# The second mixture's last 32 rows of each expert's output on four column tiles, then one summing product

## The reference

```python
gates = softmax(xf @ Wg.T);  topw, topi = top_k(gates, 2)
C = int(round(K * T * CAP_RATIO / E))          # 2 * 2048 * 1.05 / 8 = 538
...                                            # the first C tokens that chose an expert go to its buffer
h = gelu(einsum('ecd,edh->ech', buf, W1) + b1[:, None, :], approximate=False)
y = einsum('ech,ehd->ecd', h, W2) + b2[:, None, :]
...                                            # each token sums its two results, weighted by topw
```

## Time and profile before

| | us |
|---|---|
| Median of 3 runs | 2809.65 |
| Lowest and highest | 2803.67, 2810.41 |
| The profiled execution | 2807.44 |
| Its span, first to last instruction | 2806.2 |
| TensorE matmul busy in it | 2396.2 |
| VectorE, ScalarE, GpSimd busy | 1209.0, 882.0, 555.6 |

### The profile page before, as it was taken

One profiled execution on the slowest core, in us unless ns is written; L12 is line 12 of the kernel. 1 busy time (PEld: TensorE's weight loads), 2 busy tenths in 40 slices (PEclk: granted clock), 3 DMA queues, 4 the chain that ended last, 5 costly groups with the idle time before them and its releaser, 6 DMA issues.

```text
span 2806.2 us, 33074 instructions
## 1 busy us (share of the span) xinstructions
PE 2396.2 (85%) x13070; PEld 1626.3 (58%) x13070; DVE 1209.0 (43%) x2227; ACT 882.0 (31%) x2384; POOL 555.6 (20%) x553
## 2 busy tenths in 40 slices
PE   5786999938995879787999999599957899768999
PEld 5674777726773655223566657477743588623555
DVE  5753222175887563565333311300025466655220
ACT  1211222233671441553222221122214355213220
POOL 1621222234001011111344410222221100022100
PEclk9977999969997989998999999699977899979999
DMA  4006888530001000200000000322226433100000
GB/s 157 0 31 243 304 302 307 219 111 1 2 2 50 1 1 30 95 1 30 0 1 0 0 1 5 125 87 90 84 87 267 194 135 133 61 4 1 8 8 15
DMA packets 75376, 224.12 MB, mean 80 GB/s; under 512 B 9359, under 2 KB 52757, under 8 KB 65238
## 3 DMA queue, kind: packets, MB, share of 16 engines
q1 hardware_dynamic: 67894, 204.76, 20.1%
q0 software_dynamic: 7328, 17.26, 1.8%
HBM read 178.61 MB, written 45.17 MB: 80 GB/s over the span
## 4 chain that ended last, share of the span: by engine, by line
PE 48%; DVE 7%; DMA 2%; ACT 1%; POOL 1%; issue 1%; SPq 0%; POOLq 0%; DVEq 0%; ACTq 0%
PE psum L221 27%; PE psum L3246 6%; PE psum L2289 2%; PE psum L3255 2%; PE psum L2276 2%; PE psum L1786 2%; PE psum L1791 2%; DMA positions<-arena 2%; PE psum L1802 1%; DVE stats L253 1%; PE psum L1817 1%; DVE arena L2336 1%; PE psum L2506 1%; POOL small L2704 1%; PE psum L404 1%
## 5 line engine op out<-in xcount | busy, mean ns | idle before, releaser
L221 PE MATMUL psum<-arena 128*128 128x256 f32 (+6 forms) x4100 | 1046.6, 413 | 26.3 <-DVE arena L3342 13.1
L221 PEld LDWEIGHTS psum<-arena 128*128 128x128 f32 (+2 forms) x4100 | 723.8, 184 | 305.4 <-issue 136.5
L263 POOL TENSOR_SCALAR x_moments<-x_moments 128x4 f32<-128x4 f32 x48 | 12.0, 250 | 919.6 <-DVE x_moments L256 919.1
L1876 DVE TENSOR_REDUCE small<-psum 128x4 f32<-128x1024 f32 (+1 forms) x112 | 137.0, 1223 | 112.9 <-PE psum L1791 65.3
L3246 PE MATMUL psum<-arena 128*128 128x512 bf16 x768 | 166.4, 379 | 0.0
L1224 POOL DMA_INDIRECT l_out<-arena,slot_tables x79 | 78.7, 996 | 441.4 <-ACT arena L1397 233.6
L1851 ACT ACTIVATE arena<-psum,small 128x128 f32<-128x128 f32 (+1 forms) x384 | 148.9, 417 | 49.2 <-DVE small L1876 49.0
L1416 DVE TENSOR_TENSOR arena<-arena,psum 128x352 f32<-128x352 f32 x78 | 40.7, 521 | 253.3 <-ACT arena L1375 253.3
L1887 DVE COPY arena<-psum 128x512 f32<-128x512 f32 x224 | 143.6, 681 | 1.8 <-PE psum L1802 1.5
L404 PE MATMUL psum<-ident,z 128*128 128x128 f32 x256 | 48.1, 349 | 107.2 <-DVE z L274 76.7
L1786 PE MATMUL psum<-arena 32*128 32x128 f32 (+1 forms) x1280 | 133.4, 339 | 0.0
(11 more groups left out here) (334 smaller groups left out, 3389.2 us busy)
## 6 DMA issues: line engine op xcount, KB each, us to landing
arena<-L_ffn_w_in SPq DMA_DIRECT2D x39, 2176.0 KB, 8.8
arena<-L_ffn_W_in SPq DMA_DIRECT2D x16, 1024.0 KB
positions<-arena SPq DMA_DIRECT2D x16, 1024.0 KB, 6.0
arena<-positions SPq DMA_DIRECT2D x16, 1024.0 KB, 8.2
arena<-l_out SPq DMA_DIRECT2D x16, 512.0 KB, 7.3
positions<-arena SPq DMA_DIRECT2D x16, 512.0 KB, 6.5
arena<-positions SPq DMA_DIRECT2D x16, 512.0 KB, 9.0
arena<-ctx_in SPq DMA_DIRECT2D x2, 2048.0 KB, 10.1
```

Source lines behind the costliest of these rows:

```text
L221: last = nc.tensor.matmul(out, lhsT, rhs, start=(n == 0), stop=(n == len(pairs) - 1))
L1876: nc.vector.reduce_max(self.minus_top(h), use.bank(u).rearrange("p (h l) -> p h l", l=L), AX_X, negate=True).then_inc(self.topped.up(), 1)
```

## The change

The last output group of 26 rows is no longer computed as 8 products one on top of the other. In its place there are, for each expert:

- **`pe_strips(e)`**, ahead of the four full groups: 8 products for the rows 506 to 537 (32 rows, so six of the fourth group's rows are computed here too and not used). Column tile s takes the hidden tiles 2s and 2s + 1, a quarter of the features, and writes partitions 32s to 32s + 31 of one bank. The tile index is innermost.
- **A copy by ScalarE** of that bank (128 x 256) to `strips`, in two buffers by turns.
- **One summing product** behind the fourth full group: the stationary operand is `same_row`, four 32 x 32 identities on top of each other, from which the last 26 columns are taken; the moving operand is `strips`. It adds the four quarters for each of the 26 rows. VectorE adds the bias to its result as before.

`same_row` is built once, by three small additions on GpSimd at the start of the stage. Each expert now books 26 uses of PSUM instead of 25.

```diff
+        tail = k.arena[:, 4 * SLAB + 2 * 4352 + E * D:4 * SLAB + 2 * 4352 + E * D + 2 * D + 32]
+        self.strips, self.same_row = [tail[:, D * n:D * n + D] for n in (0, 1)], tail[:, 2 * D:]
+        self.folded = k.counter("same_row_made", "pool").reserve(1)
...
                 self.turn_use.append([u.add("dve", 2), u.add("act", 2)])
+            self.strip_use.append(u.add("act"))
             self.y_use.append([u.add("dve") for _ in range(RT)])
...
             pe.wait_ge(*use.emptied(self.h_use[e][1][-1]))
-            for a, u in enumerate(self.y_use[e]):
-                n = self.count(a)
-                products(nc, use.take(u)[0:n, 0:D], [(self.hid[e % 2][:, m, P * a:P * a + n], w2[:, m, :])
-                                                     for m in range(MT)]).then_inc(use.fills(u), 1)
+            self.pe_strips(e)
+            for a, u in enumerate(self.y_use[e][:-1]):
+                products(nc, use.take(u)[:, 0:D], [(self.hid[e % 2][:, m, P * a:P * a + P], w2[:, m, :])
+                                                   for m in range(MT)]).then_inc(use.fills(u), 1)
+            u, n = self.y_use[e][-1], self.count(self.RT - 1)
+            pe.wait_ge(self.folded)
+            pe.wait_ge(*use.emptied(self.strip_use[e]))
+            nc.tensor.matmul(use.take(u)[0:n, 0:D], self.same_row[:, 32 - n:32], self.strips[e % 2],
+                             start=True, stop=True).then_inc(use.fills(u), 1)
...
+    def pe_strips(self, e):
+        nc, use, u, per = self.k.nc, self.uses, self.strip_use[e], self.MT // 4
+        bank = use.take(u)
+        for j in range(per):
+            for s in range(4):
+                mm = nc.tensor.matmul(bank[32 * s:32 * s + 32, 0:D], self.hid[e % 2][:, per * s + j, CAPACITY - 32:CAPACITY],
+                                      self.w2[e % 2][:, per * s + j, :], start=(j == 0), stop=(j == per - 1))
+        mm.then_inc(use.fills(u), 1)
...
             self.empty_turn(e + 1, "act")
+            u = self.strip_use[e]
+            act.wait_ge(*use.filled(u))
+            if e >= 2:
+                act.wait_ge(*use.filled(self.y_use[e - 2][-1]))
+            copied(k, "act", self.strips[e % 2], use.bank(u)[:, 0:D]).then_inc(use.empties(u), 1)
...
     def pool(self):
+        rows = [k.ident[:, 32 * s:32 * s + 32] for s in range(4)]
+        pool.step(k.nc.gpsimd.tensor_tensor(self.same_row, rows[0], rows[1], ALU.add))
+        pool.step(k.nc.gpsimd.tensor_tensor(self.same_row, self.same_row, rows[2], ALU.add))
+        k.nc.gpsimd.tensor_tensor(self.same_row, self.same_row, rows[3], ALU.add).then_inc(self.folded.up(), 1)
         self.load_rows(0)
         self.load_rows(1)
```

More of the change, by code:

```diff
@@ L2763, in __init__ @@
         self.router = Router(k, u, self.norm, self.fetch.loaded, E * RT, CAPACITY, False)
-        self.turn_use, self.h_use, self.y_use = [[u.add("dve", 2), u.add("act", 2)]], [], []
+        tail = k.arena[:, 4 * SLAB + 2 * 4352 + E * D:4 * SLAB + 2 * 4352 + E * D + 2 * D + 32]
+        self.strips, self.same_row = [tail[:, D * n:D * n + D] for n in (0, 1)], tail[:, 2 * D:]
+        self.folded = k.counter("same_row_made", "pool").reserve(1)
+        self.turn_use, self.h_use, self.y_use, self.strip_use = [[u.add("dve", 2), u.add("act", 2)]], [], [], []
         for e in range(E):
@@ L2866, in pool @@
     def pool(self):
-        pool = self.k.pool
+        k, pool = self.k, self.k.pool
+        rows = [k.ident[:, 32 * s:32 * s + 32] for s in range(4)]
+        pool.step(k.nc.gpsimd.tensor_tensor(self.same_row, rows[0], rows[1], ALU.add))
+        pool.step(k.nc.gpsimd.tensor_tensor(self.same_row, self.same_row, rows[2], ALU.add))
+        k.nc.gpsimd.tensor_tensor(self.same_row, self.same_row, rows[3], ALU.add).then_inc(self.folded.up(), 1)
         self.load_rows(0)
         self.load_rows(1)
-        pool.wait_ge(self.k.zeroed)
+        pool.wait_ge(k.zeroed)
         for e in range(E):
```

## The result

| | before | changed |
|---|---|---|
| Median, us | 2808.30 | 2789.02 |
| Lowest and highest, us | 2803.67, 2810.41 | 2784.72, 2791.30 |
| The profiled execution's span, us | 2806.2 | 2788.3 |

The ratio is 0.9932, 95% interval 0.9914 to 0.9950, or 19.3 us by the medians. 2793 with a range of 2786 to 2801 was forecast. Both intervals hold the 16.1 us of the sum; the first, 14.0 to 24.2 us, cannot tell 16.1 from 19.3.

What follows compares the result with a forecast made beforehand. TensorE was taken to bound the kernel; 1.01 + 0.43 - 3.45 = -2.01 us an expert, -16.1 us over eight, gave 2791.4 us from the profile and 2793.6 from the median, stated as 2793, range 2786 to 2801.

Steps and rivals of the forecast that it cites:

- the sum: Per expert in the second mixture, 1.01 + 0.43 - 3.45 = -2.01 us; over eight experts -16.1 us.
- Steps 1 to 3: Per expert on TensorE: strips add 1.01 us, the summing product adds 0.43, the removed narrow group takes away 3.45.
- The signs: Marks expected in the profile after: spacing of additions, strips about 1.0 us, no wait for ScalarE, expert 31.4 to 32.0 us.
- The argument from the order of the loops: The attention block used for the strips' 1.01 us has the same order, tile index innermost.
- step 1: The strips, eight products on four column tiles ahead of the full groups: four tiles stream together, 1.01 us an expert.
- The fold at nothing: ScalarE's copy of the strips from PSUM costs nothing under four full groups; without that cover 0.5 us an expert.
- The wait for the last gelu: TensorE's wait ahead of an expert's outputs stays, standing before the strips instead of before the first full group.
- A: In the strips only two tiles run at a time: block 1.87 us, gain 1.15 an expert, -9.2 us; chance 0.08.
- B: In the strips the tiles run one after the other, each load open: block 5.2 us, +17 us; chance 0.03.
- C: TensorE's clock falls once in each expert: 2.94 us paid for 2.01 won, +7.4 us; chance 0.03.
- D: Saved TensorE work comes back as a wait, say for a bank or ScalarE: between 0 and -8 us; chance 0.06.
- 1.12 us: Alternative estimate for the strips' block from the skill page's 3.07 times, 3.45 / 3.07, giving -15.1 us in all.

Runs made afterwards that it cites:

- e11: The kernel before, with the row gathers of expert e+2 asked for only behind the last hidden product of expert e: ratio 0.9985, 2802.16 us.
- e7: The changed kernel, with the row gathers of expert e+2 asked for only behind the last hidden product of expert e: ratio 0.9931, 2786.21 us.
- e1: The changed kernel with the strips' eight products done twice for each expert, the second time over the first: ratio 0.9972, 2793.45 us.
- second comparison: The kernel before and the changed kernel, both unchanged, run once more on one chip: ratio 0.9944, 16.1 us by the medians.
- e2: The changed kernel with the tile index outermost in the strips, so a tile's two products follow each other: ratio 0.9948, 2787.41 us.
- e8: The changed kernel without the strips and without the copy by ScalarE, the summing product reading zeros: ratio 0.9919, 2782.91 us.
- e9: The changed kernel with the summing product right behind the strips, ahead of the four full groups: ratio 0.9950, 2791.96 us.
- e10: The changed kernel with the eight products on two column tiles instead of four, summed over two halves: ratio 0.9957, 2793.67 us.
- e4: The changed kernel with the strips behind the second full group instead of ahead of the first: ratio 0.9944, 2786.66 us.
- e5: The kernel before, unchanged, run and profiled once more beside the changed kernel on one chip: ratio 1.0001, 2806.39 us.
- e6: The changed kernel, unchanged, run once more on the same chip as the kernel before: ratio 0.9944, 2790.14 us.

## Why the prediction was right, and where it was loose

**Steps 1 to 3, the sum of -16.1 us.** Right. Each term was met: 1.00 us for the strips (1.01 taken), 0.54 us for the summing product with the open load that was there before (0.43 + 0.1), 3.57 us removed. The stage without its waits for gelus is 16.1 us shorter in two pairs of profiles, and in the third, e11 and e7, which has no late gelu, 16.2. The attention's block with 128 moving columns was a good stand-in for 256: e1 splits the block into 0.86 us of streaming and 0.14 of opening, as the row was split.

**The first comparison's 19.3 us** is 3 us more than the sum, and the measured 2789.0 lies 4 under the 2793. By the spans of the two profiles it is 17.9 us: 2.4 behind the stage, where the clock alone made one group 2.46 us shorter, and 0.9 ahead of it, with 1.5 us of longer waits against them. The change has no part in any of these. The other 1.4 us is within what single executions of one kernel differ by (2803.67 to 2810.41). The second comparison gives 16.1 us. That the first came out above the sum and not below it is luck.

**The signs.** Most were met: the additions stand 3.45 us apart, the last follows within 0.6 (0.55), the strips take 1.00 us, nothing waits for the fold, the clock is 1.00. One was not: an expert was to take 31.4 to 32.0 us, and five of seven took 32.1 to 32.5, because the gelus were late. With late gathers (e7) all take 31.63 or less. The distance from the stage's last addition to the first products of the next is 1.3 us longer and not as before. In the thirteen profiles it is 112.3 to 116.2 us, in the kernel before alone 112.3 to 115.3.

**The argument from the order of the loops** in step 1 was not needed. I counted it as a condition that the tile index is innermost; e2 shows that it is none.

**The fold at nothing** held, and so did the 0.5 us that it would cost without cover (e8, e9). The wait for it never showed.

**The wait for the last gelu** was "as before" in the prediction. For the structure this is right, but I took it for a fixed number. It changes from execution to execution: 2.3 and 4.4 us in two profiles of the kernel before, 0.6 where no gelu is late. It is left out of the range's working: 2.1 us between those two, and up to 3.8 where one side has late gelus and the other has none. Why an execution has them is open; the speed of the gathers, which I held for it, is not the reason.

**The rivals.** A (two tiles at a time) would have made a block of 1.87 us; e10 builds that case and finds 1.85. B (one after the other, slower) is ruled out by the same blocks. C (the clock) did not come: the block's clock is 1.00. D (the gain comes back as a wait) did not come with the change; the 1.5 us in the first pair came with the execution.

The Trainium skill's page "TensorEngine Tiling (Array Packing)", Key Properties, has the engine drained at a change of tiling mode. The additional change in e4 agrees, at 0.2 us each. The 3.07 times of the Trainium skill's page "TensorE: Matmul & The Clock Gate", Measured speedup vs the span model, stands there for four row tiles (32 of the array's rows each) with 512 moving columns; the prediction did not say so when it estimated 1.12 us for four column tiles from it (and its -15.1 us in all comes out as -15.2). The measured 1.00 us decides, 3.4 times, and it was the better choice to go by the row.

## What to carry to other kernels

Here a matmul group with 26 stationary columns cost as much as a full one (0.216 us a record). If the contraction of such a group is long, split it over four column tiles and add the quarters in one product: here 3.45 us became 1.00 + 0.43. Put the copy between the two where other products cover it, or it costs 0.5 us (e9). Before a comparison is explained to the last microsecond, take the same kernel's profile twice: here a wait that the change does not touch moved by 2 us and the next stage's clock by another 2. Before a median over a whole kernel is compared between two runs, see that it holds the same instructions in both: the 7.3 and 3.8 us of the gathers did not. And if a wait comes from work that can stand elsewhere, moving it is a cheap test: asking for the gathers half an expert later was worth 3 to 4 us in both kernels, in executions with late gelus.

## What the runs showed of the hardware

- The matmuls of different column tiles do not wait for each other in program order: with four records of one tile in a row, 16 records took 1.02 us, and with the tiles in turn 1.00.
- On two column tiles the same 16 records took 1.85 us (e10), on four 1.00; a second pass on four tiles, without a change of form, took 0.86 (e1).
- Row gathers by GpSimd took 2.8 us in the median in this stage and 7.3 in an earlier mixture of the same execution (e1). What makes the difference was not looked into.
- In seven profiles (the first two, e5, e6, e8, e9, e10), gelus of ScalarE that fall together with such gathers start mostly 1.4 to 2.1 us apart instead of 0.91, though their inputs are ready. With the gathers moved away (e7, e11) none does. In e1, e2 and e4 none does with the gathers in place. What the two share, and what differs between the executions, is open; no run here tells whether it is the engine's instruction supply, its writes or its semaphores.
